# Expert block lists by one-hot products and gathered blocks, in place of rows sorted through memory, in a decoder layer with a mixture of experts

## What is computed

```python
x = layernorm(x + self_attention(x))            # 16 heads of 16
x = layernorm(x + cross_attention(x, ctx, mask))  # ctx (2, 77, 256), 16 heads
logits = x @ Wg + bg                            # 8 experts
topk_vals, topk_idx = top_k(logits, 2)
topk_w = softmax(topk_vals)
h = relu(x @ W1[e] + b1[e]); eo = h @ W2[e] + b2[e]     # 256 -> 512 -> 256
mixed = sum over the two chosen experts of topk_w * eo
x = layernorm(x + (gamma * norm(mixed + x) + beta))
```

## Time and profile before

| | us |
|---|---|
| runs | 867.88, 879.56, 868.59; median 868.59 |
| the profiled execution | 872.9 |
| its span, first to last instruction | 871.0 |
| busy: PE, DVE, ACT, POOL | 760.3, 643.0, 459.4, 300.6 |

### The profile page before, as it was taken

The page is one execution under the profiler, slowest core; times in us unless marked ns, Lnnn a source line. Parts: engine busy times, 40 slices in busy tenths (PEclk is TensorE's granted clock), DMA queues, the critical chain, the costliest instruction groups (busy, mean ns, idle before and its releaser), DMA issues.

```text
span 871.0 us, 15027 instructions
## 1 busy us (share of the span) xinstructions
PE 760.3 (87%) x4756; PEld 377.9 (43%) x4756; DVE 643.0 (74%) x1101; ACT 459.4 (53%) x920; POOL 300.6 (35%) x249
## 2 busy tenths in 40 slices
PE   6789999999999899999988977989789999999910
PEld 3442222322222222222213445566578777777700
DVE  3488888887888887787875769889757435688657
ACT  2126677767777676777776633353344444444400
POOL 8000600000000596960002564565802753633321
PEclk9898999999999999999999999999899999999965
DMA  6746040130403599790000450000132322412121
GB/s 196 184 106 158 2 92 19 31 79 1 92 19 75 165 274 276 246 261 15 2 1 1 168 218 1 1 1 19 70 120 61 117 79 72 155 52 75 58 97 48
DMA packets 48515, 80.76 MB, mean 93 GB/s; under 512 B 16116, under 2 KB 35063, under 8 KB 47289
## 3 DMA queue, kind: packets, MB, share of 16 engines
q1 hardware_dynamic: 35017, 45.43, 19.1%
q0 software_dynamic: 9952, 31.29, 11.2%
q10 hardware_dynamic: 3472, 3.08, 1.4%
HBM read 48.21 MB, written 33.11 MB: 93 GB/s over the span
## 4 chain that ended last, share of the span: by engine, by line
PE 59%; DVE 21%; DMA 6%; issue 6%; POOL 4%; ACT 3%; SPq 1%; DVEq 0%; POOLq 0%; ACTq 0%
PE bank L534 12%; PE bank L526 11%; PE quad L507 11%; PE quad L849 8%; DVE rowmax L924 6%; PE bank L863 6%; PE bank L458 2%; ACT probs L1412 2%; POOL x_sorted L1682 2%; DVE sc L1027 1%; PE quad L604 1%; DMA kstack<-k_parts 1%; DVE max L1032 1%; PE bank L636 1%; DMA qstack<-q_parts 1%
## 5 line engine op out<-in xcount | busy, mean ns | idle before, releaser
L924 DVE TENSOR_REDUCE rowmax<-quad 128x1 f32<-128x1024 f32 x256 | 303.1, 1219 | 76.5 <-PE quad L507 75.9
L1412 ACT ACTIVATE probs<-bank 128x512 f32<-128x512 f32 x512 | 284.2, 595 | 116.3 <-PE bank L526 113.4
L526 PE MATMUL bank<-qstack,kstack 98*128 98x512 bf16 x512 | 194.0, 387 | 12.2 <-ACT probs L1412 10.2
L507 PE MATMUL quad<-kstack,qstack 96*128 96x512 bf16 x512 | 178.1, 388 | 15.7 <-DVE rowmax L924 7.4
L534 PE MATMUL bank<-probs,v_all 128*32 128x512 f32 x1024 | 139.1, 611 | 0.0
L526 PEld LDWEIGHTS bank<-qstack,kstack 98*128 98x128 bf16 x512 | 48.9, 97 | 191.4 <-ACT probs L1412 160.2
L849 PE MATMUL quad<-xbT,w_all 128*128 128x128 bf16 x1104 | 100.4, 226 | 8.1 <-issue 4.4
L849 PEld LDWEIGHTS quad<-xbT,w_all 128*128 x1104 | 76.9, 97 | 33.0 <-issue 17.3
L1736 POOL DMA_INDIRECT y_tokens<-ysb,dest x46 | 49.0, 1066 | 97.4 <-DVE ysb L1164 87.4
L507 PEld LDWEIGHTS quad<-kstack,qstack 96*128 96x128 bf16 x512 | 48.6, 99 | 77.4 <-DVE rowmax L924 39.8
L1526 ACT ACTIVATE xbT<-bank 128x512 bf16<-128x512 bf16 x46 | 27.4, 597 | 96.9 <-PE bank L830 96.9
(11 more groups left out here) (173 smaller groups left out, 964.9 us busy)
## 6 DMA issues: line engine op xcount, KB each, us to landing
w_all<-w_split SPq DMA_DIRECT2D x2, 4096.0 KB, 18.0
xb<-x_sorted SPq DMA_DIRECT2D x46, 129.0 KB, 2.1
x_sorted<-blank POOLq DMA_DIRECT2D x6, 774.0 KB, 8.8
w1raw<-in_w POOLq DMA_DIRECT2D x8, 512.0 KB, 5.9
w2raw<-in_w POOLq DMA_DIRECT2D x8, 512.0 KB, 5.6
w_split<-w1two POOLq DMA_DIRECT2D x8, 512.0 KB, 5.1
w_split<-w2two POOLq DMA_DIRECT2D x8, 512.0 KB, 3.5
q_parts<-parts SPq DMA_DIRECT2D x24, 128.0 KB
```

The source lines that it names most:

```text
L507: mm = pe.matmul(bank[2 * (p % 2) + e], q, kstack[slot][0:MAXROW, j, e * 512:e * 512 + 512], start=True, stop=True)
L526: mm = pe.matmul(bank[4 + i % 2], kstack[slot][0:KROWS, j, kt * P:kt * P + P], qstack[slot][0:KROWS, half, j, :], start=True, stop=True)
L924: dve.tensor_reduce(rowmax[:, k % 2, p:p + 1], quad[:, 2 * (p % 2):2 * (p % 2) + 2, :].rearrange("p a n -> p (a n)"), AX_X, ALU.max).then_ ...
L1412: act.activation(probs[:, i % PR, :], bank[4 + i % 2], ACT.Exp, scale=INV4).then_inc(probs_ready, 1)
```

## The change

The rows of a half are no longer sorted through memory. DVE compares each token's row number with all positions: for each of 16 columns (choice and tile) it makes a 128 x 128 one-hot of the position within a block (onehot) and a 23-wide one-hot of the block, times the token's tile (1 to 8, or 33 to 40 for the second choice) and times its partition (entry). PE adds up 16 products, onehot turned times entry; the result has for each position and block the number of the token that belongs there, or zero. DVE makes of it the index of the row to read (source) and of the row to write (dest) for all blocks of the half. SP stores the bf16 rows of a group in token order, and POOL gathers each block with an indirect DMA, six blocks ahead. The fills, the scatters, the tags, SP's block loads and the DVE operation per block go away. The wait of PE's turn_last is for lists_taken instead of tab_done.

```diff
-        xs = [nc.dram_tensor(f"x_sorted{h}", (XROWS, XW), F32, kind="Internal").ap() for h in range(2)]
+        xs = [nc.dram_tensor(f"x_rows{h}", (S, 2 * D), BF16, kind="Internal").ap() for h in range(2)]
-        iota = sb("iota", [P, HB])
-        slots = sb("slots", [P, NT])
+        iota = sb("iota", [P, P])
+        marks = sb("marks", [P, 2, QS])
+        cross_w = sb("cross_w", [P, 4, C2, D])
+        w_in.update({n: cross_w[:, i, :, :] for i, n in enumerate(("cwq", "cwk", "cwv", "cwo"))})
+        onehot = cross_w[:, 1:3, :, :].rearrange("p a c d -> p (a c d)").bitcast(BF16).rearrange("p (q r) -> p q r", q=QS)
-        xsend = attn_all[:, :].rearrange("p (n d) -> p n d", d=XW)
-        xrow = attn_all[:, :].bitcast(BF16).rearrange("p (n d) -> p n d", d=2 * XW)
-        tag = xsend[:, :, D:XW]
+        xrow = attn_all[:, :].bitcast(BF16).rearrange("p (n d) -> p n d", d=2 * D)
...
-        rowf = sb("rowf", [P, 2, NT])
-        rowof = sb("rowof", [P, 2, NT], U32)
+        rowf = sb("rowf", [P, 2, HT])
+        which = sb("which", [P, QS, HB], BF16)
+        entry = sb("entry", [P, QS, 2, HB], BF16)
+        source = sb("source", [P, 2, HB], U32)
-        dest = sb("dest", [P, XB], U32)
+        dest = sb("dest", [P, 2, HB], U32)
...
+        LISTS = bank[3][:, 400:400 + 2 * HB]
-        FETCHED = HB + 9
-        SPREAD1 = [5 + j // 2 if j < HT else 1 + j for j in range(2 * HT)]
...
-            def load_block(m):
-                h, i = m // HB, m % HB
-                if i == 0:
-                    sp.wait_ge(scattered[h], 16 * 2 * HT)
-                if m >= XB:
-                    sp.wait_ge(xb_turned, m - XB + 1)
-                    sp.wait_ge(dest_done, m - XB + 1)
-                sp.dma_start(xb32[:, m % XB, :], xs[h][i * P:(i + 1) * P, :]).then_inc(xb_loaded[m % XB], 16)
+            def store_rows(g):
+                sp.wait_ge(xlow_done, 4 * g + 4)
+                rows_ = xs[g // 2].rearrange("(n p) d -> p n d", p=P)[:, 4 * (g % 2):4 * (g % 2) + 4, :]
+                sp.dma_start(rows_, xrow[:, 4 * g:4 * g + 4, :]).then_inc(rows_stored[g // 2], 16)
             def store_tiles(g):
-            sp.wait_ge(s2_ready, NT)
-            sp.wait_ge(q2_ready, 2 * TG)
-            for m in range(LEAD):
-                load_block(m)
+            for g in range(2):
+                store_rows(g)
-            for m in range(LEAD, BLOCKS):
-                load_block(m)
-                if m == FETCHED:
-                    await_outputs(sp, 0)
-                    for i in range(HT // 2):
-                        load_outputs(sp, 0, i)
+            for g in range(2, TG):
+                store_rows(g)
+            await_outputs(sp, 0)
+            for i in range(HT // 2):
+                load_outputs(sp, 0, i)
...
-                    pe.wait_ge(tab_done, 1)
+                    pe.wait_ge(lists_taken, 1)
+            def lists(h):
+                pe.wait_ge(onehot_done, h + 1)
+                pe.wait_ge(s2_taken, NT)
+                for q in range(QS):
+                    mm = pe.matmul(LISTS, onehot[:, q, :], entry[:, q, :, :].rearrange("p k b -> p (k b)"), start=(q == 0), stop=(q == QS - 1))
+                mm.then_inc(lists_ready, 1)
...
                 elif n in (NT - 3, NT - 1):
                     for half in range(2):
                         values2(g, half, slice((i - 1) * P, (i + 1) * P))
+                elif n == NT - 2:
+                    lists(0)
             turn_x2(TG - 2)
             logits2(TG - 2)
                 elif m == 4:
                     rank(2)
                     rank(3)
+                elif m == 7:
+                    lists(1)
 ...
-                dve.tensor_copy(tag[:, tiles, 0], slots[:, tiles])
-                dve.tensor_copy(tag[:, tiles, 1], topf[:, tiles, 0])
             def place(h):
-                link(dve.tensor_reduce(rowf[:, :, tiles], spots[:, :, :, :], AX_X, ALU.add))
-                dve.tensor_copy(rowof[:, :, tiles], rowf[:, :, tiles]).then_inc(row_done, 1)
+                link(dve.tensor_reduce(rowf[:, :, :], spots[:, :, :, :], AX_X, ALU.add))
+            def make_onehot(h):
+                row = rowf[:, :, :].rearrange("p j n -> p (j n)")
+                shifted, rounded, blk, pos = (third[:, i, :] for i in range(4))
+                link(dve.tensor_scalar(shifted, row, -(P - 1) / 2, 1.0 / P, ALU.add, ALU.mult))
+                link(dve.tensor_scalar(rounded, shifted, ROUND, None, ALU.add))
+                link(dve.tensor_scalar(blk, rounded, -ROUND, None, ALU.add))
+                link(dve.scalar_tensor_tensor(pos, blk, -float(P), row, ALU.mult, ALU.add))
+                if h:
+                    dve.wait_ge(lists_ready, h)
+                dve.tensor_tensor(onehot, iota[:, :].rearrange("p (o r) -> p o r", o=1).to_broadcast([P, QS, P]),
+                                  pos.rearrange("p (q o) -> p q o", o=1).to_broadcast([P, QS, P]), ALU.is_equal)
+                link(dve.tensor_tensor(which[:, :, :], iota[:, 0:HB].rearrange("p (o b) -> p o b", o=1).to_broadcast([P, QS, HB]),
+                                       blk.rearrange("p (q o) -> p q o", o=1).to_broadcast([P, QS, HB]), ALU.is_equal))
+                for k in range(2):
+                    en = dve.tensor_tensor(entry[:, :, k, :], which[:, :, :],
+                                           marks[:, k, :].rearrange("p (q o) -> p q o", o=1).to_broadcast([P, QS, HB]), ALU.mult)
+                en.then_inc(onehot_done, 1)
+            def read_lists(h):
+                high, low, second, tile, token, empty = (listed[:, i, :] for i in range(6))
+                dve.wait_ge(lists_ready, h + 1)
+                dve.tensor_copy(listed[:, 0:2, :], LISTS.rearrange("p (k b) -> p k b", k=2)).then_inc(lists_taken, 1)
+                dve.wait_ge(lists_taken, h + 1)
+                dve.tensor_scalar(empty, high, 0.0, FULL, ALU.is_equal, ALU.mult)
+                link(dve.tensor_scalar(second, high, 32.0, None, ALU.is_gt))
+                link(dve.scalar_tensor_tensor(tile, second, -32.0, high, ALU.mult, ALU.add))
+                link(dve.scalar_tensor_tensor(token, tile, float(P), low, ALU.mult, ALU.add))
+                dve.tensor_scalar(source[:, h, :], token, -float(P), 0.0, ALU.add, ALU.max).then_inc(lists_done, 1)
+                link(dve.scalar_tensor_tensor(tile, token, 2.0, second, ALU.mult, ALU.add))
+                dve.scalar_tensor_tensor(dest[:, h, :], tile, -2.0 * P, empty, ALU.add, ALU.add).then_inc(lists_done, 1)
             def weigh(h):
-            def send_rows(m):
-                h, i, r = m // HB, m % HB, m % XB
-                dve.wait_ge(xb_loaded[r], 16 * (m // XB) + 16)
-                dve.scalar_tensor_tensor(dest[:, r:r + 1], xtag[:, r, 1:2], table[:, h, i:i + 1], xtag[:, r, 0:1],
-                                         ALU.not_equal, ALU.add).then_inc(dest_done, 1)
             def split_hidden(m):
...
                     sum_probs(n + 2)
                     if g == TG - 1:
                         last_divide(n + 2)
+                        read_lists(0)
                 elif i in (0, 3) and 1 < n + 1 < NT:
                     sum_probs(n + 1)
                 if i == 0 and g:
                     take(n + FAR)
                 if n + FAR == NT - 1:
                     last_shift()
+                    make_onehot(0)
                 if n + FAR in SCORED:
                     top_two(SCORED.index(n + FAR))
              for m in range(BLOCKS):
-                send_rows(m)
                 split_hidden(m)
                 if m:
                     keep_y(m - 1)
                     top_two(TG - 1)
                 elif m == 5:
                     place(1)
+                elif m == 6:
+                    make_onehot(1)
+                elif m == 8:
+                    read_lists(1)
                 elif m == 7:
                     weigh(1)
                 for g in range(2):
...
-            def fill_sorted(h, i):
-                lo, hi = i * HB // FILLS, (i + 1) * HB // FILLS
-                pool.dma_start(xs[h].rearrange("(r p) c -> p r c", p=P)[:, lo:hi, :],
-                               blank[:, :].rearrange("p (o c) -> p o c", o=1).to_broadcast([P, hi - lo, XW])).then_inc(filled[h], 16)
-            pool.wait_ge(zeros_set, 1)
-                fill_sorted(e // FILLS, e % FILLS)
-            for h in range(2):
-                pool.wait_ge(filled[h], 16 * FILLS)
             def root(k, lo, hi):
...
-            def scatter(n, j):
-                h = n // HT
-                pool.wait_ge(row_done, h + 1)
-                pool.wait_ge(xlow_done, n + 1)
-                pool.indirect_dma_start(xs[h], bass.IndirectOffsetOnAxis(ap=rowof[:, j, n:n + 1], axis=0), xsend[:, n, :], None).then_inc(scattered[h], 16)
             def over_heads(v):
...
-                if n == NT - 5:
-                    for k in range(2):
-                        for j in range(2):
-                            scatter(k, j)
```

(32 more changed lines are left out.)

31 lines of the change are left out of this document (13 added, 18 removed).

## The result

The changed kernel took 876.11 us in the median of 20 runs (872.97 to 880.86), the kernel before 872.47 in 20 runs beside them (867.13 to 879.56): a ratio of 1.005, 95% interval 1.0031 to 1.0069. It is 3.6 us slower. In three later comparisons the ratio was 1.0038 [1.0011, 1.0066], 1.0031 [1.0005, 1.0058] and 1.0048 [1.0019, 1.0076]. Ratios and medians leave out four slow runs of the later jobs (882.0, 972.1 and 1058.8 us of before, 1451.4 of move_spread_lead8). The three runs of before that the forecast started from had a median of 868.59; with 17 more it is 872.47, and the profiled execution, at 872.9, was a typical one and not 4.3 us too slow.

The account below looks back on a forecast made before the run. PE was taken as the bound, with 59% of the chain of waits. The terms -2.5 + 2.0 + 0.4 + 0.9 + 0.1 - 0.7 gave +0.2 us on 872.9, carried over to a median of 868.8; range 862.5 to 875.5.

Parts of the forecast that it names:

- The base: Starting time: the profiled execution, 872.9 us, was taken as 4.3 above the median of the runs, 868.59.
- Part 1: Attention: without eight fill DMAs the K load PE waits for near 345 us lands sooner; -2.5 us, bounds 0 and 3.3.
- Part 2: Seam from cross attention to block 0: make_onehot(0) on DVE delays the last division, +2.0 us, and lower clock, +0.4.
- The clock term: Seam: PE's gap moves to some 5 us ahead of 624.8, lower clock reaches the last tile's transposes; +0.4 us.
- Part 3: Expert blocks, paced by PE: lists(1) in PE's queue +0.9 us, make_onehot(1) +0.1; POOL's gather and send 2.7 of 4.0.
- just fits: Block 7: its split, behind make_onehot(1), ends at about 678.4 and PE wants it at 678.49; +0.1 us, up to 2.4.
- rival D: First gathers come late because rows or lists are not ready; needs 5 us, then one for one, say 872; chance 0.03.
- the step on POOL: Blocks: POOL issues a gather and a send per block, 2.7 us of 4.0 with gaps, so PE keeps the pace.
- Part 4: End of the blocks, 778 to 818 us: about six L1143 of 0.13 us leave the chain through DVE; -0.7 us.
- Rival B: Seam: DVE's one-hot on the path, slower than before; 875.9 us with a slow product, 871.3 with fills giving nothing; chance 0.24.
- Rival A: Attention: K load's wait and clock dip go whole, -3.3 us, and the seam costs 1.5 less; 866.0 us; chance 0.22.
- C: Blocks: POOL becomes the bound, gather and send 2.24 us each beside DVE work, 5.1 us a block; about 919; chance 0.03.

Follow-up runs that it names:

- move_spread_lead8: Changed kernel with make_onehot(0) behind the last tile's division, make_onehot(1) cut in two, gathers eight blocks ahead: 876.95 us (ratio to before 1.0025) and 870.45 (0.9976).
- after_fills: Changed kernel with the eight fill DMAs put back, into buffers that nobody reads: 877.93 us, ratio to the kernel before 1.0074.
- before_third: A repeat of the unchanged kernel before, for its profile; last rden to place(0)'s first comparison took 112.4 us, in the other seven profiles 107.2 to 109.0.
- 4: Changed kernel with make_onehot(0) moved behind the last tile's division, read_lists(0) and lists(0) later too; two runs: 876.03 us (ratio to before 1.005), 878.15 (1.0036).
- 7: Changed kernel, make_onehot(0) moved and make_onehot(1) cut in two: 871.88 us (ratio to before 0.9997), 872.81 (0.9995); with gathers eight blocks ahead 876.95, 870.45.
- LEAD 8: Changed kernel with gathers issued eight blocks ahead in POOL's order instead of six; alone 877.61 us, ratio to the kernel before 1.0048.
- the cut: Changed kernel with make_onehot(1) split over blocks 6 and 7, lists(1), weigh(1), read_lists(1) one block later; alone 875.69 us, ratio to before 1.005.

## Why the prediction was wrong

The forecast was +0.2 us on the profiled execution and no change; measured +2.8 between the means of four profiles, and 2.1 to 3.6 between medians. That it is within 2% was right. By its own steps:

- **The base.** "4.3 above the median of the runs" was a draw of three. This moved the predicted time by 4 us, and is why 876.1 lies outside 862.5 to 875.5.
- **Part 1, the fills (-2.5): the term that was mis-sized.** Measured -0.6 between the four pairs, -1.6 over twenty profiles, neither clear of their scatter. The step that failed is that without the fills the load would land the 1.6 us sooner that it needs: it took 11.6 us on average before and 11.5 after, and PE still waits 0.8 to 1.9 us for kstack. And the clock dip behind it, in the forecast a cost of every execution, is absent from two of the four profiles of before.
- **Part 2, the seam (+2.0 and +0.4).** Each duration came as worked out: the comparison 2.29 us (2.3), make_onehot(0) 4.52 (4.6), L971's excess of 1.5 gone, POOL's gathers 1.0 each, block 0 turned without a wait. The seam is +2.8 over the mean of before when the clock recovers. The clock term was mis-sized: +0.4 holds for three of the eight profiles with make_onehot(0) in this place and the gap left empty; in one the low clock cost 1.3 us more (5.87 less 4.59) and in four 2.7 to 2.8. The text moved one gap of 5 us ahead of the last tile; there are two, the old one of 2.2 us and a new one of 3.2 ahead of tile 14, and the clock falls behind both.
- **Part 3, the blocks (+1.0).** Measured +1.0 up to block 7, -0.15 from 7 to 20, and +1.0 from 20 to 28, so +1.9. make_onehot(1) "just fits" was right on PE (0.24 us of wait, +0.14 between two blocks), and lists(1) took 0.40 us of PE, not 0.9. The term that was missing is the late gather, at nothing in the sum: the gather of block 29 lands 7.0 to 8.3 us after its issue where PE waits for it. It is rival D's mechanism, though in the middle of the blocks and not at the first: gathers stand behind add_beta and sends in POOL's queue, which the step on POOL counted only in busy time, and beside the yg loads, which it left out.
- **Part 4 (-0.7).** -0.4 from block 28 to 45.
- **Not in the sum.** From the last ysb to the end 0.9 us more, all behind DVE's last instruction (5.1 us before the end in before, 6.2 in after). The place is POOL's DRAIN (L77) in the closing of the program, which every other engine waits for. Of before and then of after:

```profile
L77 POOLq DRAIN  x1: 7915/7915/7915, 862.9 to 862.9; - x1
```

```profile
L77 POOLq DRAIN  x1: 8975/8975/8975, 861.9 to 861.9; - x1
```

It begins beside POOL's last operation (861.99 in after) and ends 0.2 us before the span does; SP, with the output stored, is through 1.2 us before it in before and 2.2 to 2.4 in the changed kernels. It took 7.91 us in all four profiles of before, 8.98 in the fifteen of changed kernels without fills and 9.06 in after_fills. POOL issues 78 indirect and 40 direct DMAs in before, 92 and 32 in after, 92 and 40 in after_fills. That the DRAIN grows with the indirect ones fits these three figures; no run changes their number alone, so it isn't shown.

Rival B had the place and the sign: DVE's one-hot on the path, one for one, with "the fills giving nothing" at 871.3, which is +2.7. Its condition of a slow product was not needed. That +2.7 is so near +2.8 is luck in part, since B had neither the late gather nor the DRAIN, and the measured difference has the -1.0 of before_third in it. Rival A's relief didn't come. C was wrong: gathers average 1.01 us, and the longest, issued at 673.24 beside L1137, took 2.00. D, the late gather, took part as said.

That the seam's loss is DVE's one-hot ahead of the last divisions is shown: moved away, the stretch is 36.0 to 37.7 us instead of 39.3 to 42.3 in five profiles (4 and 7), and 39.1 in a sixth, where PE waits 4.2 for the first gather. lists(0) and read_lists(0) were moved with it, but lists(0) stood in PE's wait for the last division and read_lists(0) behind that division, so they were not on the way. No run makes the one-hot longer in its place, so "one for one" is read from the rows and not tried. LEAD 8 is shown for its stretch, and the cut for 0.3 us. That together they give the whole loss back is shown on one chip (7). Open are what lengthens the DRAIN, what the fills cost, and the long blocks of two chips; the low clock's share of the typical run is known only as an estimate, about 1 us.

## What to carry to other kernels

Work that replaces a path through memory is not free because it is short: here 4.5 us on VectorE replaced 27 us of scatters that had cost the seam some 2.5 (0.8 of PE's wait, 1.7 on DVE), and landed on the one engine whose next two instructions everyone waited for. Put it behind the last instruction that others need, in pieces shorter than the slack between two of them, and issue gathers so early that one late landing doesn't show. Before a wait is booked as a gain, check in a second execution whether the transfer behind it changed at all. For changes of half a per cent, take several profiles of both kernels and subtract stretch by stretch before sizing any term; a wait or a clock dip seen in one execution is a chance and not a cost.
